# A two-layer decoder on one NeuronCore: loads across two stage borders, a band mask by quadrant products, and a mask by selection with one product on GpSimd

## Chip, cores and metric

One core of one Trainium2 chip runs the whole program, eight stages one after the other in a single launch. The metric is device time in microseconds (us) of one execution. Engines: TensorE (PE), VectorE (DVE), ScalarE (ACT), GpSimd (POOL); SyncE (SP) and ScalarE issue the transfers. Each engine works through its own instruction list in order and waits on semaphores for the others.

## What is computed

Input x is 32 sequences of 128 tokens with 256 features (4,096 tokens), and a context of the same size. Two decoder layers follow. The parts that matter here:

```python
# layer 0, self attention: g = x Wg + bg, v = x Wv + bv, 16 heads of 16
corr = g.g / (|g||g| + 1e-8), masked (j <= i);  corr = (corr + 1) / 2
denom = mean(corr, keys) + 0.5
fitness = 1 / (denom * sum(1 / denom, queries))
p = softmax(corr * fitness where j <= i else -1e10);  x = layernorm(x + (p v) Wo)
# layer 0, cross attention: 16 heads of 16, keys within 64 of the query (the band mask)
# layer 0, feed forward: one quantised 256x256 product
# layer 1, gated attention (Mega): a long convolution over the sequence axis of 32,
#   mx = silu(conv(xn) + omega xn), then attention of 128 queries, 512 values
# layer 1, cross attention: keys and values of width 1,024 from the context
# layer 1: 8 experts, 2 per token
```

## The kernel before, in words

Everything is float32 but for the masks, the identities for them and the quantised product. A tile is 128 tokens, so there are 32 tiles. The stages, with their functions: `l0_attn` (project, then `l0_attn_heads`), `l0_xattn`, `l0_ffn`, `mega_conv`, `mega_attn`, `l1_xattn` and `moe_experts`. A stage ends with all its transfers landed and its semaphores cleared; then all engines begin the next.

**Self attention, heads** (`l0_attn_heads`, lines 237 to 567). Each tile is handled in two halves u = 0, 1 of eight heads. Per tile: GpSimd pads the operands (L318), TensorE transposes them (L448), ScalarE copies them out, TensorE makes correlations and a guard (L461), ScalarE takes a tanh of the guard (L540), VectorE multiplies to the correlation c (L384), GpSimd adds a mask of -1e30 above the diagonal into cm (L324, 327), VectorE sums rows (L400), inverts, TensorE sums the inverses over queries (L477), VectorE makes the fitness (L411) and multiplies cm by it (`weigh`, L393), ScalarE takes the exponential (L546), TensorE transposes it in four groups (L483) that ScalarE copies (L552), TensorE applies it to the values and to ones (L496), VectorE divides (L418), TensorE multiplies by Wo (L514), VectorE adds the residual (L426). The order on each engine is written out by hand: a `walk` over steps s in which each part, with a lag, works on tile s - lag. A wait `slot_free(sem, n, depth)` waits until item n - depth has left the buffer.

**Cross attention of layer 0** (`l0_xattn`, from L569). Groups of four tiles; per tile TensorE first writes the band mask into the score banks (identity times `bandb`, L761: two products of 512 columns per half), then adds the scores (L765), and so on through maximum, exponential, row sum, and a product with the inverse sum on GpSimd (L663) from e into en, which TensorE transposes (L779).

**Keys and values of layer 1** (class `EarlyKeysValues`, L912) depend on the context alone. They are made in 144 pieces, nine per group of two tiles (a transposition of the context, four of keys, four of values), in gaps of the feed forward stage and of the convolution: `make` on TensorE (L957), `keep` on ScalarE (L998). Two banks are used in turn, so a piece waits until the one before the last is kept. In `l0_ffn` one piece stands ahead of the first group (`FFN_FIRST = 1`) and five go with each of eight groups; in `mega_conv` 40 stand ahead of the convolution (`CONV_AFTER`), 8 between its products and the rest behind it. The weights (2 MB) and the first two context loads are issued in `l0_ffn`.

**Convolution** (`mega_conv`). SP loads parameters and xn (L1373), stores the kernel in 32 shifted copies to HBM (`toep`, L1376), waits for these stores, and loads four Toeplitz tiles back (L1381). TensorE multiplies (L1455), ScalarE takes the silu (L1410), SP stores mx (L1385).

**Gated attention** (`mega_attn`). SP first loads group 0 of mx and xn (L1545), then 13 weights and tables (L1558 to 1566). VectorE, ScalarE and TensorE wait for all 13.

## Time and profile before

| what | value |
|---|---|
| median of three runs | 2716.57 us (2715.59 to 2717.06) |
| the profiled execution | 2716.16 us |
| its span | 2714.4 us, 44,490 instructions |
| TensorE busy | 2370.4 us (87%) |
| VectorE busy | 1388.5 us (51%) |
| ScalarE busy | 1126.6 us (42%) |
| GpSimd busy | 874.9 us (32%) |

Busy shares are averages over stages with different limits, so a stage has to be read by itself. PEld is TensorE's loading of the stationary operand, which overlaps its products. In a row of the timeline the bracket tells how long the engine was idle before and what ended it; "issue" means nothing that the profile shows.

### The profile page before, as it was taken

How to read it: one execution, taken by the hardware profiler on the slowest of the kernel's cores; microseconds unless marked ns; L12 is line 12 of the kernel's file. 1: busy time of each engine (PE TensorE's matmuls, PEld its weight loads, DVE VectorE, ACT ScalarE, POOL GpSimd, SP SyncE). 2: the span in 40 equal slices, each digit the busy share in tenths (PEclk: the TensorE clock that was granted, in tenths of full speed). 3: DMA queues.
4: the chain of work that ended last, by engine and by line, in shares of the span. 5: the costliest groups of instructions: out<-in, count | busy, mean ns of one | idle time of the engine just before them, and what ended most of it. 6: DMA issues, size and time to landing. Idle time of an engine off the chain costs nothing. (4 is left out here: it accounts for less than half of the span.)

```text
span 2714.4 us, 44490 instructions
## 1 busy us (share of the span) xinstructions
PE 2370.4 (87%) x17103; PEld 1816.2 (67%) x17134; DVE 1388.5 (51%) x2497; ACT 1126.6 (42%) x1930; POOL 874.9 (32%) x850
## 2 busy tenths in 40 slices
PE   9688888699996668996989959999997799999994
PEld 4466666466664445754656648888886688888883
DVE  5598998477876850002354436877877111111113
ACT  2456666356564544432332315555564111111113
POOL 2455555144444680000010013544544122222221
PEclk9699999899999889997999979999998899999997
DMA  2143444510101649454111032233232766566634
GB/s 74 48 109 105 113 119 114 129 32 24 48 9 36 219 166 242 121 189 130 31 55 39 24 126 86 94 109 122 98 101 88 264 193 180 179 187 193 181 102 136
DMA packets 214465, 313.23 MB, mean 115 GB/s; under 512 B 63856, under 2 KB 196848, under 8 KB 201072
## 3 DMA queue, kind: packets, MB, share of 16 engines
q1 hardware_dynamic: 190992, 253.95, 30.7%
q0 software_dynamic: 14304, 18.69, 3.8%
q10 hardware_dynamic: 8960, 37.75, 3.6%
q8 instruction: 138, 2.26, 0.3%
q14 instruction: 71, 0.58, 0.1%
HBM read 187.58 MB, written 122.76 MB: 114 GB/s over the span
## 5 line engine op out<-in xcount | busy, mean ns | idle before, releaser
L2569 ACT ACTIVATE me_h<-me_ps_h 128x512 f32<-128x512 f32 x156 | 93.1, 597 | 454.1 <-PE me_ps_h L2549 454.1
L2607 DVE TENSOR_SCALAR me_yo<-me_ps_y,moe_xg 128x256 f32<-128x256 f32 x78 | 37.7, 484 | 476.3 <-PE me_ps_y L2558 410.0
L2497 POOL DMA_INDIRECT xo<-me_yo,me_row x78 | 121.8, 1562 | 441.5 <-DVE me_yo L2607 407.3
L2549 PE MATMUL me_ps_h<-me_xt,me_w 128*128 128x256 f32 x1024 | 226.3, 379 | 0.0
L2558 PE MATMUL me_ps_y<-me_w,me_h 128*128 128x256 f32 x1024 | 226.1, 379 | 0.0
L2558 PEld LDWEIGHTS me_ps_y<-me_w,me_h 128*128 128x128 f32 x1024 | 194.6, 190 | 26.5
L2549 PEld LDWEIGHTS me_ps_h<-me_xt,me_w 128*128 128x128 f32 x1024 | 192.1, 190 | 24.8
L327 POOL TENSOR_TENSOR l0ah_cm<-l0ah_c,l0ah_after 128x1024 f32<-128x1024 f32 x64 | 151.7, 2370 | 174.4 <-DVE l0ah_c L389 174.4
L2038 POOL TENSOR_TENSOR l1x_e<-l1x_e,l1x_ri 128x1024 f32<-128x1024 f32 x64 | 121.7, 1901 | 235.4 <-DVE l1x_ri L2322 235.4
L663 POOL TENSOR_TENSOR l0x_en<-l0x_e,l0x_ri 128x1024 f32<-128x1024 f32 x64 | 120.0, 1895 | 208.9 <-DVE l0x_ri L885 208.9
L984 PE MATMUL kv_ps<-kv_w_v,kv_ct 128*128 128x512 f32 x256 | 120.3, 610 | 21.6 <-PEq L82 12.4
L977 PE MATMUL kv_ps<-kv_ct,kv_w_k 128*128 128x256 f32 x512 | 121.8, 395 | 9.5 <-ACT kv_va L1023 6.2
L544 ACT ACTIVATE l0ah_f<-l0ah_ps_s 128x1024 f32<-128x1024 f32 x64 | 65.6, 1025 | 142.8 <-PE l0ah_ps_s L473 142.8
L2157 PE MATMUL l1x_ps_p<-l1x_xct,l1x_w_q 128*128 128x256 f32 x512 | 123.5, 385 | 0.0
L2195 PE MATMUL l1x_ps_o<-l1x_w_o,l1x_ot 128*128 128x256 f32 x512 | 120.4, 389 | 1.4 <-ACT l1x_ot L2268 1.4
L977 PEld LDWEIGHTS kv_ps<-kv_ct,kv_w_k 128*128 128x128 f32 x512 | 100.9, 199 | 30.5 <-ACT kv_va L1023 7.4
L2258 ACT ACTIVATE l1x_e<-l1x_sx 128x1024 f32<-128x1024 f32 x64 | 67.4, 1053 | 115.7 <-DVE l1x_sx L2313 115.6
L844 ACT ACTIVATE l0x_et<-l0x_ps_e 128x512 f32<-128x512 f32 x128 | 69.9, 595 | 99.0 <-PE l0x_ps_e L779 98.7
L1662 DVE TENSOR_SCALAR ma_zq<-ma_zp 128x1 f32<-128x1 f32 x1 | 0.2, 152 | 211.7 <-DMA ma_same<-in_msame 211.7
L2195 PEld LDWEIGHTS l1x_ps_o<-l1x_w_o,l1x_ot 128*128 128x128 f32 x512 | 95.9, 192 | 15.7 <-ACT l1x_ot L2268 1.7
L2319 DVE TENSOR_REDUCE l1x_rs<-l1x_e 128x8 f32<-128x1024 f32 x64 | 78.0, 1219 | 49.0 <-ACT l1x_e L2258 48.5
L2157 PEld LDWEIGHTS l1x_ps_p<-l1x_xct,l1x_w_q 128*128 128x128 f32 x512 | 93.5, 192 | 12.6 <-ACT l1x_xct L2243 0.3
(387 smaller groups left out, 5344.5 us busy)
## 6 DMA issues: line engine op xcount, KB each, us to landing
me_w<-in_w SPq DMA_DIRECT2D x32, 2048.0 KB, 9.5
xs<-dec_zero SPq DMA_DIRECT2D x31, 1032.0 KB, 7.0
k<-kv_kt ACTq DMA_DIRECT2D x16, 1024.0 KB, 6.0
v<-kv_va ACTq DMA_DIRECT2D x16, 1024.0 KB, 6.0
l1x_kt<-k SPq DMA_DIRECT2D x16, 1024.0 KB, 4.9
l1x_va<-v SPq DMA_DIRECT2D x16, 1024.0 KB, 5.6
moe_w_first<-in_w SPq DMA_DIRECT2D x7, 2048.0 KB, 10.3
moe_xg<-xs SPq DMA_DIRECT2D x39, 258.0 KB, 2.8
```

What stands on the lines that cost most here:

```text
L327: pool.tensor_tensor(cm[:, n % 2, u, :, :], c[:, u, :, :], after[:, :].unsqueeze(1).to_broadcast([P, HALF, P]), ALU.add).then_inc(corr_mas ...
L663: pool.tensor_tensor(en[:, n % 2, u, :, :], e[:, n % 2, u, :, :], spread(ri[:, n % 2, u, :], P), ALU.mult).then_inc(e_scaled, 1)
L977: ins = pe.matmul(bank[:, c * self.GP:(c + 1) * self.GP], self.w_k[:, k, at], self.ct[:, g % 2, k, :], start=k == 0, stop=k == 1)
L984: ins = pe.matmul(bank[:, :], self.ct[:, g % 2, k, t * P:(t + 1) * P], self.w_v[:, k, 512 * c:512 * c + 512], start=k == 0, stop=k == 1)
L2038: pool.tensor_tensor(e[:, n % 2, u, :, :], e[:, n % 2, u, :, :], spread(ri[:, n % 2, u, :], P), ALU.mult).then_inc(e_scaled, 1)
L2157: last = pe.matmul(ps_p[i % 2][:, c * GP:(c + 1) * GP], w_q[:, k, at], xct[:, k, :], start=k == 0, stop=k == 1)
L2195: last = pe.matmul(ps_o[:, 0:2, :].rearrange("p a b -> p (a b)"), ot[:, c, :], w_o[:, c, :], start=c == 0, stop=c == C - 1)
L2319: dve.tensor_reduce(rs[:, n % 2, u, :], e[:, n % 2, u, :, :], AX.X, ALU.add).then_inc(summed, 1)
L2497: pool.indirect_dma_start(token_rows, bass.IndirectOffsetOnAxis(row[:, j % 2, q:q + 1], 0), yo[:, j % 2, q, :], None, compute_op=ALU.add). ...
L2549: last = pe.matmul(ps_h[i % HB][:, f % 2, :], weights(j)[:, FFN * c + f * P:FFN * c + f * P + P], xt[:, j % 2, c, :], start=c == 0, stop=c ...
L2558: last = pe.matmul(ps_y[q][:, 0:D], h[:, j % 2, f, q * P:(q + 1) * P], weights(j)[:, W2 + D * f:W2 + D * f + D], start=f == 0, stop=f == F ...
L2569: act.activation(h[:, j % 2, 2 * i:2 * i + 2, :], ps_h[i % HB][:, :, :], ACT.Gelu).then_inc(gelued, 1)
```

## The change

Self attention: the mask is no longer added to c. The product with the fitness reads c itself; the exponential is made without a mask, and GpSimd then sets it to zero above the diagonal, in place, with two selects per tile. The product for u = 1 moves from VectorE to GpSimd, which gets its fitness from a buffer fs of its own. The order on all engines is new. Cross attention: the band is added behind the scores, only where it can be nonzero, by products of 64 rows, 64 output partitions and 4 x 64 columns; the product with the inverse sum is made in place. The key and value weights and first contexts are loaded in the cross attention; ten pieces stand ahead of the feed forward's first group. The gated attention's weights and its first xn are loaded within the convolution, between the stores of `toep` and the loads of the Toeplitz tiles, and its first mx at that stage's end. Some of its tiles are laid over buffers of `EarlyKeysValues`.

```diff
@@ l0_attn_heads, GpSimd
-                def mask_corr(n, u):
-                    item_done(pool, corr_done, 2 * n + u)
-                    slot_free(pool, weighted, 2 * n + u, 4)
-                    pool.tensor_tensor(cm[:, n % 2, u, :, :], c[:, u, :, :], after[:, :].unsqueeze(1).to_broadcast([P, HALF, P]),
-                                       ALU.add).then_inc(corr_masked, 1)
+                def weigh_odd(n):
+                    item_done(pool, fit_done, n)
+                    item_done(pool, corr_done, 2 * n + 1)
+                    slot_free(pool, exped, n, 1, 2)
+                    pool.tensor_tensor(wt[:, 1, :, :], c[:, n % 2, 1, :, :], spread(fs[:, n % 2, :], P), ALU.mult).then_inc(weighted1, 1)
+
+                def mask_e(n, u):
+                    item_done(pool, exped, 2 * n + u)
+                    pool.affine_select(out=e[:, n % 2, u, :, :], in_=e[:, n % 2, u, :, :], compare_op=ALU.is_ge, fill=0.0, base=0,
+                                       pattern=[[0, HALF], [-1, P]], channel_multiplier=1).then_inc(masked, 1)
-                walk([(4, last_of_group(roots)), (3, bias_x), (0, lambda n: mask_corr(n, 0)), (-1, pads), (0, lambda n: mask_corr(n, 1))])
+                walk([(-2, pads), (1, lambda n: mask_e(n, 0)), (1, lambda n: mask_e(n, 1)), (2, last_of_group(roots)), (0, bias_x), (0, weigh_odd)])
@@ l0_attn_heads, VectorE
-                def weigh(n, u):
-                    i = 2 * n + u
+                def weigh_even(n):
                     item_done(dve, fit_done, n)
-                    item_done(dve, corr_masked, i)
-                    slot_free(dve, exped, i, 2)
-                    dve.tensor_tensor(wt[:, u, :, :], cm[:, n % 2, u, :, :], spread(small(3)[:, HALF * u:HALF * u + HALF], P), ALU.mult).then_inc(weighted, 1)
+                    slot_free(dve, exped, n, 1, 2)
+                    dve.tensor_tensor(wt[:, 0, :, :], c[:, n % 2, 0, :, :], spread(small(3)[:, 0:HALF], P), ALU.mult).then_inc(weighted0, 1)
-                walk([(0, lambda n: correlate(n, 0)), (3, residual), (1, lambda n: weigh(n, 0)), (1, lambda n: weigh(n, 1)), (0, lambda n: correlate(n, 1)), (0, row_sums),
-                      (2, divide), (0, fitness)])
+                walk([(1, weigh_even), (0, lambda n: correlate(n, 1)), (2, divide), (0, row_sums), (2, residual), (-1, lambda n: correlate(n, 0)), (0, fitness)])
@@ l0_attn_heads, TensorE
-                    item_done(pe, exped, 2 * n + j // 2)
+                    item_done(pe, masked, 2 * n + j // 2)
-                walk([(3, multiply), (0, lambda n: score(n, 1)), (2, lambda n: transpose_e(n, 0)), (2, lambda n: transpose_e(n, 1)),
-                      (2, lambda n: transpose_e(n, 2)), (2, lambda n: transpose_e(n, 3)), (-1, transposes), (2, apply), (-1, lambda n: score(n, 0)),
-                      (0, sum_inverse)])
+                walk([(3, multiply), (2, lambda n: transpose_e(n, 0)), (1, sum_inverse), (2, lambda n: transpose_e(n, 1)), (2, lambda n: transpose_e(n, 2)), (2, lambda n: transpose_e(n, 3)), (0, lambda n: score(n, 1)), (2, apply), (-1, transposes), (-1, lambda n: score(n, 0))])
@@ l0_attn_heads, ScalarE
-                walk([(0, lambda n: guard(n, 1)), (2, copy_et), (7, normalise), (-1, copy_ops), (1, lambda n: exponentials(n, 0)),
-                      (1, lambda n: exponentials(n, 1)), (-1, lambda n: guard(n, 0))])
+                walk([(0, copy_ops), (2, lambda n: exponentials(n, 1)), (0, lambda n: guard(n, 0)), (7, normalise), (2, copy_et), (0, lambda n: guard(n, 1)), (1, lambda n: exponentials(n, 0))])
@@ l0_xattn, GpSimd: the product in place, ScalarE's wait
-                        pool.tensor_tensor(en[:, n % 2, u, :, :], e[:, n % 2, u, :, :], spread(ri[:, n % 2, u, :], P),
+                        pool.tensor_tensor(e[:, n % 2, u, :, :], e[:, n % 2, u, :, :], spread(ri[:, n % 2, u, :], P),
-                    slot_free(act, e_scaled, n, 2, 2)
+                    slot_free(act, e_transposed, n, 2, 4)
@@ l0_xattn, SP
+                    if g + 3 == NG:
+                        kv.load_weights(sp)
+                        for early in range(2):
+                            kv.load_ctx(sp, early)
@@ l0_xattn, TensorE, score
-                        for q in range(2):
-                            pe.matmul(ps_s[u][:, q, :, :], identb[:, :], bandb[:, :, :], start=True, stop=False)
                         for c in range(2):
                             for q in range(2):
                                 at = slice(32 * (2 * u + q), 32 * (2 * u + q) + 32)
-                                last = pe.matmul(ps_s[u][:, q, 2 * c:2 * c + 2, :], qt[at, g % 2, c, t * P:(t + 1) * P],
-                                                 kt[at, g % 2, c, :, t * P:(t + 1) * P], start=False, stop=c == 1)
+                                pe.matmul(ps_s[u][:, q, 2 * c:2 * c + 2, :], qt[at, g % 2, c, t * P:(t + 1) * P],
+                                          kt[at, g % 2, c, :, t * P:(t + 1) * P], start=c == 0, stop=False)
+                        for q in range(2):
+                            for lo in range(2):
+                                rows64, keys64 = slice(64 * lo, 64 * lo + 64), slice(64 - 64 * lo, 128 - 64 * lo)
+                                last = pe.matmul(ps_s[u][rows64, q, :, keys64], identb[rows64, rows64], bandb[rows64, :, keys64],
+                                                 start=False, stop=True)
@@ l0_ffn
-FFN_FIRST, FFN_STEP = 1, 5
+FFN_FIRST, FFN_STEP = 10, 5
-                kv.load_weights(sp)
...
-                for g in range(2):
-                    kv.load_ctx(act, g)
...
+                kv.keep(act, 0, 2)
                 sum_squares(0)
                 act.wait_ge(w_loaded, 5 * 16)
                 act.activation(w[:, :, :], w_i[:, :, :], ACT.Copy).then_inc(w_ready, 1)
-                kv.keep(act, 0, FFN_FIRST)
+                kv.keep(act, 2, 5)
                 sum_squares(1)
+                kv.keep(act, 5, FFN_FIRST)
@@ mega_conv, SP
                                  kp[:, :, L - 1 - l:2 * L - 1 - l]).then_inc(pad_stored, 16)
+                mw.load_weights(sp)
+                mw.load(sp, 0, xn, 0)
                 sp.wait_ge(pad_stored, 16 * L)
...
                 sp.wait_ge(stored, 16 * G)
+                mw.load(sp, 1, mx_out, 0)
@@ mega_attn, SP: load(0) and the 13 weight loads are gone; tiles over the buffers of kv
+        v = kv.kt[:, :, :, :].rearrange("p u (t c) n -> p u t (c n)", t=G)
+        r = kv.va[:, :, :, :].rearrange("p u t (c n) -> p u (t c) n", c=2)
+        hr = kv.w_kv[:, :, :, :].rearrange("p u k (c m n) -> p u (k c) m n", c=2, m=4)
```

## Rows read from the trace of the kernel before

**Rows 1.** Busy time by stage, columns as headed.

```profile
core 0: us, PE busy (x) PEld busy (x) DVE busy (x) ACT busy (x) POOL busy (x), PEclk, DMA share, GB/s
...
72.00:500.00 428.00, 342.12 (x5312) 268.33 (x5312) 353.23 (x454) 245.53 (x358) 217.24 (x237) 0.93 0.42 106
500.00:879.00 379.00, 336.79 (x2657) 218.54 (x2688) 275.96 (x323) 207.73 (x338) 153.44 (x112) 0.97 0.12 38
```

**Rows 2.** Timeline (start us, us, engine, line), self attention, about one tile.

```profile
303.29 0.54 PEld L467 LDWEIGHTS l0ah_ps_s<-l0ah_ops 16*128 16x128 f32 x16 [0.20 <-issue]
...
305.15 0.40 PE L481 MATMUL l0ah_ps_a<-l0ah_st,l0ah_ones 128*128 128x16 f32 x2
...
305.29 1.02 ACT L544 ACTIVATE l0ah_f<-l0ah_ps_s 128x1024 f32<-128x1024 f32 x1 [0.70 <-PE l0ah_ps_s L473]
...
306.34 1.22 DVE L389 SCALAR_TENSOR_TENSOR l0ah_c<-l0ah_f,l0ah_ps_s 128x1024 f32<-128x1024 f32 x1 [0.28 <-ACT l0ah_f L544]
...
308.50 2.35 DVE L398 TENSOR_TENSOR l0ah_wt<-l0ah_cm,l0ah_ps_a 128x1024 f32<-128x1024 f32 x2
...
311.37 1.12 PE L493 MATMUL l0ah_ps_e<-l0a_ident,l0ah_e 128*128 128x128 f32 x8 [0.70 <-ACT l0ah_et L556]
...
312.02 2.29 DVE L402 TENSOR_REDUCE l0ah_st<-l0ah_c 128x16 f32<-128x2048 f32 x1
...
313.29 0.65 PE L504 MATMUL l0ah_ps_e<-l0ah_et,l0a_va 128*32 128x128 f32 x16
...
314.55 0.26 DVE L409 RECIPROCAL l0ah_st<-l0ah_ps_a 128x16 f32<-128x16 f32 x1
...
315.31 1.76 DVE L421 RECIPROCAL l0ah_rd<-l0ah_ps_e 128x256 f32<-128x256 f32 x1 [0.50 <-PE l0ah_ps_e L510]
...
317.10 0.42 DVE L424 TENSOR_TENSOR l0ah_ot<-l0ah_ps_e,l0ah_rd 128x256 f32<-128x256 f32 x1
...
318.22 1.22 DVE L389 SCALAR_TENSOR_TENSOR l0ah_c<-l0ah_f,l0ah_ps_s 128x1024 f32<-128x1024 f32 x1 [0.28 <-ACT l0ah_f L544]
```

**Rows 3.** Timeline, cross attention: from one tile's multiply to its transposes.

```profile
645.16 0.73 PEld L800 LDWEIGHTS l0x_ps_e<-l0x_w_o,l0x_ot 128*128 128x128 f32 x4 [0.20 <-issue]
...
647.71 0.11 PEld L761 LDWEIGHTS l0x_ps_s<-l0x_bandb,l0x_identb 128*128 128x128 bf16 x2 [0.33 <-issue]
...
648.25 0.73 PEld L765 LDWEIGHTS l0x_ps_s<-l0x_kt,l0x_qt 32*128 32x128 f32 x8 [0.42 <-issue]
...
649.31 0.86 PEld L779 LDWEIGHTS l0x_ps_e<-l0x_ident,l0x_en 128*128 128x128 f32 x8 [0.33 <-issue]
```

**Rows 4.** Timeline, feed forward: its first transposes and VectorE's first residual.

```profile
897.03 1.01 PE L1239 MATMUL ffn_ps_t<-ffn_identb,ffn_xq 128*128 128x128 bf16 x8 [11.91 <-DVE ffn_xq L1289]
...
904.15 1.65 DVE L1298 SCALAR_TENSOR_TENSOR ffn_r<-ffn_ps_y,ffn_st,ffn_xb 128x256 f32<-128x256 f32 x4
```

**Rows 5.** Timeline, gated attention: its first loads, copies and projection.

```profile
1222.55 2.85 SPq L1545 DMA_DIRECT2D ma_xin<-mx  x4
...
1234.93 0.47 SPq L1566 DMA_DIRECT2D ma_same<-in_msame  x1
...
1242.25 1.08 ACT L1603 ACTIVATE ma_xt<-ma_ps_t 128x512 f32<-128x512 f32 x2 [24.82 <-DMA ma_same<-in_msame]
...
1245.74 3.78 PE L1807 MATMUL ma_ps_z<-ma_xt,ma_w_z 128*128 128x512 f32 x4 [0.38 <-DVE ma_bm L1679]
```

**Rows 6.** Groups of instructions on GpSimd: busy us, mean ns, idle before.

```profile
L327 POOL TENSOR_TENSOR l0ah_cm<-l0ah_c,l0ah_after 128x1024 f32<-128x1024 f32 x64 | 151.7, 2370 | 174.4 <-DVE l0ah_c L389 174.4
...
L663 POOL TENSOR_TENSOR l0x_en<-l0x_e,l0x_ri 128x1024 f32<-128x1024 f32 x64 | 120.0, 1895 | 208.9 <-DVE l0x_ri L885 208.9
```

**Rows 7.** The same view, a select on GpSimd.

```profile
L642 POOL TENSOR_SCALAR_AFFINE_SELECT l0x_band<-l0x_band 128x512 f32<-128x512 f32 x1 | 0.6, 641 | 0.1
```

**Rows 8.** Timeline, convolution: its first product, and pieces of keys behind it.

```profile
1084.61 3.84 PE L1455 MATMUL mc_ps<-mc_xg,mc_t 128*128 128x128 f32 x16 [6.33 <-DMA mc_t<-toep]
...
1173.40 7.07 PE L977 MATMUL kv_ps<-kv_ct,kv_w_k 128*128 128x256 f32 x32
...
1188.13 7.07 PE L977 MATMUL kv_ps<-kv_ct,kv_w_k 128*128 128x256 f32 x32
```

More of the change, by code:

```diff
@@ L922, in __init__ @@
         self.ident = kit.sb("ident", [P, P])
[L923 removed]
+        self.w_kv = kit.sb("w_kv", [P, 2, 2, H * self.W])
+        self.w_k, self.w_v = self.w_kv[:, 0, :, :], self.w_kv[:, 1, :, :]
         self.b_k = kit.sb("b_k", [P, self.C])
@@ L928, in __init__ @@
         self.va = kit.sb("va", [P, 2, self.G, H * self.W])
-        self.ps = [kit.ps(f"ps{i}", [P, 2 * self.GP]) for i in range(2)]
         self.k_loaded, self.v_loaded = kit.sem("k_loaded"), kit.sem("v_loaded")
@@ L935, in __init__, with take_banks @@
         self.kit = kit
+    def take_banks(self, kit):
+        self.ps = [kit.ps(f"ps_kv{i}", [P, 2 * self.GP]) for i in range(2)]
     def piece(self, n):
@@ L1525, in mega_attn @@
          normed) = (kit.sem(n) for n in names)
-        xin_loaded = [[kit.sem(f"{c}_loaded{u}") for u in range(2)] for c in ("xn", "mx")]
         x_loaded = [kit.sem(f"x_loaded{u}") for u in range(3)]
@@ L1542, in load @@
                     slot_free(sp, xt_ready, g, 2, 4)
-                    for c, src in ((1, mx_in), (0, xn_in)):
-                        for t in range(G):
-                            sp.dma_start(xin[:, g % 2, c, t, :], tiles(src)[G * g + t, :, :, :]).then_inc(xin_loaded[c][g % 2], 16)
+                    mw.load(sp, 1, mx_in, g)
+                    mw.load(sp, 0, xn_in, g)
                 def load_x(g):
```

131 lines of the change are left out of this document (73 added, 58 removed).

## The prediction

> **What bounds the kernel now.** I read the stage windows first, because the 44,490 instructions fall into stages that run one after the other, then the timeline of one period inside each stage that the diff touches, then the borders. In the self attention's head stage VectorE is busy 353 of 428 us and TensorE 342; in the cross attention TensorE is busy 337 of 379 and VectorE 276 [rows 1]. So the first is a cycle between engines with VectorE as its fullest member, the second runs at TensorE's order. The reader is to see in the timeline that one tile of the head stage takes 318.22 - 306.34 = 11.88 us [rows 2]. In the cross attention the same TensorE steps repeat with idle gaps of 0.2 to 0.4 us, the longer ones at a change of matmul form [rows 3]. At the borders two idle stretches stand out: TensorE sits 11.9 us before the first transposes of the FFN [rows 4], and the gated attention, though its first input has landed, starts its copies only at 1242.25, when the last of 13 weight loads has landed, 24.8 us after ScalarE went idle [rows 5].
>
> **Sum is made against the profiled execution:** 2716.16 us, with a span of 2714.4; the median of the runs is 2716.57, so 0.4 more. 0.2% is 5.4 us, about what a measurement of this kernel can tell from no change.
>
> **Self attention, heads.** Removed: two GpSimd additions of 2.37 us per tile and the copy cm; one VectorE product (two take 2.35 us) goes to GpSimd [rows 2, 6]. Added on GpSimd: one product of the same form as the cross attention's, 1.90 us [rows 6], and two selects over 128x1024 in place. The trace has a select over 128x512, 0.64 us [rows 7]; twice that, 1.28, is my value, with 0.64 and 2.37 (the addition, same size) as ends. GpSimd's sum for these falls from 4.74 to 1.90 + 2.56 = 4.46 us of 11.9: it is on no bound. VectorE falls from 353/32 = 11.0 to about 10 us a tile, but what closes the period is the new order, so I walked it. From TensorE's sum of inverses: that product 0.40; one group of four transposes 0.55; its bank's copy before the last group may start, about 0.75 (the row shows 0.70 of such idle); the last group 0.5; together 2.2. The score of half u=1, until tanh starts: 305.29 - 303.29 = 2.00. Tanh, until the correlation starts: 306.34 - 305.29 = 1.05. The correlation 1.22, less 0.07 overlap. Divide, which now stands ahead of the row sums: 317.10 - 315.31 + 0.42 = 2.2 (its input, the apply product, takes 315.31 - 313.29 = 2.02 after the score and is ready by then). Row sums until the inverse is there: 314.55 + 0.26 - 312.02 = 2.79. Signal back to TensorE 0.13. Sum 11.5 us, against 11.88: 0.38 x 32 tiles = **-12 us** [rows 2]. GpSimd is not in this cycle, nor is the moved product: the even product (1.2) and the odd one run beside the score. Ends: TensorE's own 342/32 = 10.7 us a tile would give -38; a tenth of a microsecond missed in the walk's other direction, with the gain gone, +3. The earlier addition of x and bias has a load issued a whole tile ahead, so I cost it at nothing; a late load would hold GpSimd's queue, the odd product with it, and GpSimd has 11.5 - 4.46 - 2.0 = 5 us of room a tile, so only what passes those counts.
>
> **Cross attention.** Per half the band's two 512-column products take 648.25 - 647.71 = 0.54 us, loads and streaming; a half's score takes 649.31 - 648.25 = 1.06 before another form may start; and a tile's multiply, band, score take 647.71 - 645.16 = 2.55 [rows 3]. Afterwards four 256-column products per half stand behind the score. Streaming alone is 0.54 - 0.11 = 0.43 for 1,024 columns, so 0.107 for each product of 256. If the two diagonal quadrants of one pair run side by side, a half's band is 0.21 plus 0.11 to 0.2 of load and drain, 0.33 to 0.42. Multiply then changes straight to the narrow form, 0.73 + 0.33. A tile is 1.06 + 2 x 1.06 + 2 x 0.37 = 3.9 against 649.31 - 645.16 = 4.15: 0.22 x 32 = **-7 us** (ends -4 and -10). TensorE's order is the bound, so this passes through; VectorE has 3 us of room a tile. The product in place on GpSimd changes no duration, and ScalarE's new wait on the transposes is already met, as the same engine copies those banks earlier in the same step. Two megabytes of key and value weights and two context loads are issued here now, behind the last input load, with nothing but stores behind them: 0; without cover it would be one store a few microseconds late, with two buffers of four tiles to absorb it.
>
> **FFN head.** Nine more pieces of keys and values are made before the first group. Nine pieces (one group of two tiles) take 1188.13 - 1173.40 = 14.73 us [rows 8]. They fill the 11.9 us idle and the start moves forward by the context load that is no longer waited for. The first transposes come some 4 us later, yet VectorE takes up the first product only at 904.15, after its own work, with no idle before it [rows 4]; that leaves room, which I put at 2 to 3 us. I take **0** (-1 to +3).
>
> **Convolution.** Nine pieces leave its tail, which TensorE bounds: -14.7 [rows 8]. Against that, SP now issues 13 weight loads and 4 loads of xn before the four loads of the Toeplitz tiles. In the gated attention 8 input and 13 weight loads took 1234.93 + 0.47 - 1222.55 = 12.85 us to issue, 0.61 each, so 17 take 10.4 [rows 5]; about 1 of it lies in the wait for its stores that SP has there in any case: +9.4. TensorE already waits 6.3 us for these tiles [rows 8], so the whole delay shows. The 3.4 MB also go ahead of the tiles in the same queue: there, 3.9 MB were in after 1242.25 - 1222.55 = 19.7 us, so 3.4 MB would take 17, most of it beside the issue. Ends +6 and +17. Stage: -14.7 + 9.4 = **-5.3**. The stores of mx move with it and have 46 pieces, 46 x 14.73 / 9 = 75 us, behind them as cover; uncovered, they would give back the rest of the 14.7.
>
> **Gated attention.** Its 13 weights, xn and mx of group 0 have landed. The stage's first instruction is at 1222.55; identity, four groups of transposes with their copies, and the small products need about 5.9 us, so its first projection starts at about 1228.4 instead of 1245.74: -17.3 [rows 5]. The 5.9 is 1245.74 - 1242.25 = 3.5 from the first copy on, plus the first two groups of transposes and the identity, which used to lie in the wait. Some of the first products also leave the slow clock earlier, so **-18** (-16 to -20). The tiles borrowed from the keys' buffers are written after those stores were waited for. One more clearing of semaphores: +0.4.
>
> **Sum:** -12 - 7 + 0 - 5.3 - 18 + 0.4 = -41.9: 2716.2 - 41.9 = **2674 us**.
>
> **Rivals.**
> *The quadrants do not run side by side.* Both write one bank, while the scores' two row groups q, which the kernel of before runs as a pair, go to separate banks. Then a half's band is 0.43 + 0.11 to 0.2, a tile 1.06 + 2.12 + 1.2 = 4.35 against 4.15: +6 instead of -7, so 2687. The Trainium skill, TensorEngine Tiling (Array Packing), section Restrictions and Gotchas, says that different row tiles cannot access the same PSUM bank simultaneously; by it this rival holds. No run here shows it. What speaks for overlap is that the pairs differ in output partitions too. Chance 0.3.
> *The weights delay the Toeplitz tiles further.* If the 3.4 MB drain at their old pace and the tiles follow only then, beside the keys' stores, the convolution starts 17 to 23 us late instead of 9.4, about 20: 2685. For: the 19.7 us above. Against: SP's issue overlaps the drain, and the keys' traffic stops once TensorE idles. Chance 0.1. The Trainium skill, DMA: Bandwidth & Descriptors, section Queues, rings and completion order, says that each engine takes a row's descriptors in ring order; with that the drain is in front, not beside.
> *The head stage's order closes tighter*, near TensorE's 10.7: 2650 to 2660. Against: the walk above. Chance 0.07.
> *Slower: GpSimd becomes the bound of the head stage.* Its place: two selects a tile ahead of the odd product on one in-order engine. With s for a select, its tile is 2s + 1.90 + 2.0 of other work (217/32 - 4.74) [rows 1, 6]. It decides above s = 3.8 us, where that passes 11.5; the whole gain is spent at about s = 4.45. At s = 5 the tile is 13.9: 2.4 x 32 = +77 on the sum: 2751. Against: 0.64 us for half the size [rows 7]. Chance 0.03.
> *It doesn't do what it says:* TensorE's first projection still waits, for mx of group 0 or another load: the 18 are lost: 2692. The load of mx is issued after its stores, with tens of microseconds of pieces behind. Chance 0.03.
> The forecast, as summed, has 0.47.
>
> **How the numbers follow.** The likeliest case alone spans 2665 to 2683. To leave out no more than 2 in 10 the range takes in the serial quadrants and the later tiles with their ends, and the tighter order in part: 2656 to 2697. Faster by over 0.2% (below 2711) is every case but the GpSimd bound and a pile of bad ends: 0.94; same 0.03; slower 0.03.
>
> **What would show it.** Head stage: period near 11.5 us, divide ahead of the row sums, selects near 1.3 us. Cross attention: the gap from a half's score to the next form, near 0.37 or 0.6. Convolution: its idle before the first product near 16 us instead of 6.3, its tail 14.7 shorter. Gated attention: first projection 6 us after the stage's start. A head stage not faster, or TensorE idle for over 25 us ahead of the convolution, would make the prediction wrong.

## The result, and the profile after

The changed kernel takes 2681.57 us in the median of four executions (2678.93 to 2689.17), the kernel before 2716.08: a ratio of 0.9876, with a 95% interval of 0.9859 to 0.9893, or 34.5 us less. The forecast was 2674, with a range of 2656 to 2697, and 0.94 for faster by over 0.2%. The profiled execution is the longest of the four, 2689.17 us with a span of 2687.4. Against the profiled execution before (2716.16) it gained 27.0 us, and the stages below account for those 27.0, not for the median's 34.5.

Busy time by stage in the profile after; columns as headed, and a stage runs from its own first instruction to the next one's.

```profile
core 0: us, PE busy (x) PEld busy (x) DVE busy (x) ACT busy (x) POOL busy (x), PEclk, DMA share, GB/s
80.30:506.30 426.00, 355.55 (x5312) 277.30 (x5312) 308.00 (x448) 252.46 (x355) 197.25 (x270) 0.90 0.41 107
506.30:878.30 372.00, 331.32 (x2816) 219.45 (x2816) 275.97 (x323) 207.96 (x338) 153.59 (x113) 0.96 0.14 46
878.30:1010.20 131.90, 99.37 (x424) 66.68 (x425) 93.33 (x233) 73.40 (x180) 94.68 (x109) 0.90 0.55 193
1010.20:1221.60 211.40, 183.07 (x664) 125.85 (x664) 5.43 (x11) 87.69 (x157) 7.14 (x4) 0.94 0.71 189
1221.60:1564.70 343.10, 297.54 (x1282) 205.93 (x1282) 156.08 (x290) 113.38 (x168) 27.73 (x29) 0.98 0.15 47
```

| stage | before, start to start | after | change | forecast |
|---|---|---|---|---|
| self attention, heads | 421.3 | 426.0 | +4.7 | -12 |
| cross attention | 378.3 | 372.0 | -6.3 | -7 |
| feed forward | 130.5 | 131.9 | +1.4 | 0 |
| convolution | 212.3 | 211.4 | -0.9 | -5.3 |
| gated attention | 368.7 | 343.1 | -25.6 | -18 |

The later stages are as before within 0.5 us. Stage by stage, the profiled execution gained 15 us less than the forecast 41.9: the head stage is 16.7 us longer than forecast and the convolution 4.4, while the gated attention gained 7.6 us more than it should. Two large errors work against each other, and the median, 7.6 us below the profiled execution, lies nearer to the forecast than these stages do.

**The head stage's period is the one that was walked out.** Timeline of one tile after, the rows that answer to [rows 2]:

```profile
306.92 0.40 PE L486 MATMUL l0ah_ps_a<-l0ah_st,l0ah_ones 128*128 128x16 f32 x2 [0.64 <-DVE l0ah_st L412]
...
309.25 0.73 PE L472 MATMUL l0ah_ps_s<-l0ah_ops 16*128 16x128 f32 x16
...
311.25 1.02 ACT L547 ACTIVATE l0ah_f<-l0ah_ps_s 128x1024 f32<-128x1024 f32 x1 [1.29 <-PE l0ah_ps_s L478]
...
312.30 1.22 DVE L394 SCALAR_TENSOR_TENSOR l0ah_c<-l0ah_f,l0ah_ps_s 128x1024 f32<-128x1024 f32 x1 [1.68 <-POOL l0ah_wt L328]
...
313.44 1.75 DVE L427 RECIPROCAL l0ah_rd<-l0ah_ps_e 128x256 f32<-128x256 f32 x1
...
315.56 2.28 DVE L405 TENSOR_REDUCE l0ah_st<-l0ah_c 128x16 f32<-128x2048 f32 x1
...
318.09 0.26 DVE L412 RECIPROCAL l0ah_st<-l0ah_ps_a 128x16 f32<-128x16 f32 x1
...
318.40 0.40 PE L486 MATMUL l0ah_ps_a<-l0ah_st,l0ah_ones 128*128 128x16 f32 x2 [0.64 <-DVE l0ah_st L412]
```

From one sum of inverses to the next it is 318.40 - 306.92 = 11.48 us. The walk's seven steps measure: transposes 2.33 us (forecast 2.2), score 2.00, tanh 1.05 and row sums to inverse 2.79 (all three as forecast), correlation 1.14 (forecast 1.15), divide 2.12 (forecast 2.2), and signal 0.05 (forecast 0.13). The bracket at 312.30 names GpSimd's product, whose end falls there by chance: the same product of the next tile ends at 322.83, and that tile's correlation starts only at 323.78, when its tanh is done.

**And yet the stage is longer**, because five of its tiles are much longer. In each, TensorE stands still in the middle of a run of transposes. TensorE's products at one of these places:

```profile
275.40 0.27 PE L463 MATMUL l0ah_ps_a<-l0a_ident,l0ah_rpad 128*128 128x128 f32 x1
275.51 0.27 PE L462 MATMUL l0ah_ps_a<-l0a_ident,l0ah_lpad 128*128 128x128 f32 x1
278.27 0.33 PE L463 MATMUL l0ah_ps_a<-l0a_ident,l0ah_rpad 128*128 128x128 f32 x1 [2.48 <-issue]
...
281.57 2.08 PE L525 MATMUL l0ah_ps_e<-l0ah_w_o,l0ah_ot 128*128 128x256 f32 x4
```

The same stretch by engine, four microseconds each:

```profile
272.00:276.00 4.00, 3.78 (x95) 2.87 (x91) 2.33 (x3) 2.17 (x3) 2.93 (x5) 1.00 1.09 275
276.00:280.00 4.00, 1.48 (x22) 1.12 (x23) 3.97 (x3) 1.37 (x3) 0.62 (x1) 1.00 0.08 16
280.00:284.00 4.00, 4.00 (x29) 3.07 (x28) 0.84 (x4) 2.17 (x3) 1.09 (x1) 0.58 0.00 0
```

The reader should see three things. The product at 278.27 carries no wait ("issue"), and its twin at 275.40 ran without pause. The DMA engines are full (share 1.09) in the 4 us ahead: a zero store of 1 MB was issued at 270.66. And behind the gap the granted clock falls to 0.58, near the lower level of 1.2 GHz, so that the output product takes 2.08 us instead of the 1.13 that it takes elsewhere. The five tiles take 13.7, 14.4, 14.8, 15.1 and 16.6 us from row sums to row sums instead of 11.49, standstill and slow clock together. (One more, near the stage's start, takes 13.6 us with no gap: there the granted clock is at the lower level until 116.8 us.) The kernel before has no such gap in this stage; behind its first tiles only two are stretched, by 1.1 us each.

**Cross attention, convolution, gated attention.** The quadrants in the cross attention, after:

```profile
641.08 0.14 PEld L773 LDWEIGHTS l0x_ps_s<-l0x_bandb,l0x_identb 64*64 64x64 bf16 x4 [0.33 <-issue]
641.42 0.86 PEld L787 LDWEIGHTS l0x_ps_e<-l0x_ident,l0x_e 128*128 128x128 f32 x8 [0.20 <-issue]
```

A half's band takes 641.42 - 641.08 = 0.34 us, where [rows 3] had 0.54. SP's loads at the border, the convolution's first product, and the first two projections of the gated attention, after:

```profile
1072.09 0.47 SPq L950 DMA_DIRECT2D mw_w_z<-in_mwz  x1
...
1081.79 3.69 SPq L964 DMA_DIRECT2D mw_xin<-xn  x4
...
1085.61 8.15 SPq L1441 DMA_DIRECT2D mc_t<-toep  x4
...
1098.13 2.07 PE L1516 MATMUL mc_ps<-mc_xg,mc_t 128*128 128x128 f32 x8 [19.70 <-DMA mc_t<-toep]
...
1226.86 1.98 PE L1843 MATMUL ma_ps_z<-ma_xt,mw_w_z 128*128 128x512 f32 x4 [0.39 <-DVE ma_bm L1715]
...
1256.54 1.88 PE L1843 MATMUL ma_ps_z<-ma_xt,mw_w_z 128*128 128x512 f32 x4
```

The 17 loads hold SP for 1085.61 - 1072.09 = 13.5 us, and TensorE now waits 19.7 us for the Toeplitz tiles, where [rows 8] had 6.33 and the forecast near 16. The gated attention's first projection starts 5.3 us after the stage, as against 23.2 [rows 5].

### The profile page after: what moved, and what is told of

The parts are those of the page before. It is cut to its first block and busy times, and to the rows that moved or that the text cites. A ratio compares the mean times of both kernels' runs of the same rounds, so it can differ in the third digit from the quotient of the medians.

```text
span 2687.4 us, 44698 instructions
## 1 busy us (share of the span) xinstructions
PE 2370.5 (88%) x17262; PEld 1822.0 (68%) x17262; DVE 1349.1 (50%) x2497; ACT 1136.7 (42%) x1930; POOL 855.7 (32%) x882
## 5 line engine op out<-in xcount | busy, mean ns | idle before, releaser
L664 POOL TENSOR_TENSOR l0x_e<-l0x_e,l0x_ri 128x1024 f32<-128x1024 f32 x64 | 120.1, 1897 | 201.7 <-DVE l0x_ri L893 201.7
L394 DVE SCALAR_TENSOR_TENSOR l0ah_c<-l0ah_f,l0ah_ps_s 128x1024 f32<-128x1024 f32 x64 | 77.2, 1207 | 74.9 <-ACT l0ah_f L547 66.5
L1043 PE MATMUL mc_ps_kv<-kv_w_kv,kv_ct 128*128 128x512 f32 x176 | 83.3, 616 | 16.8 <-PEq L82 14.0
L332 POOL TENSOR_SCALAR_AFFINE_SELECT l0ah_e<-l0ah_e 128x1024 f32<-128x1024 f32 x64 | 69.9, 1094 | 87.8 <-ACT l0ah_e L553 87.2
L2346 DVE TENSOR_REDUCE l1x_top<-l1x_ps_s 128x8 f32<-128x1024 f32 x64 | 77.6, 1213 | 39.4 <-PE l1x_ps_s L2204 38.5
L559 ACT ACTIVATE l0ah_et<-l0ah_ps_e 128x512 f32<-128x512 f32 x128 | 73.7, 596 | 54.1 <-PE l0ah_ps_e L498 53.2
```

The lines of the kernel that those rows point to most:

```text
L394: dve.scalar_tensor_tensor(out=c[:, n % 2, u, :, :].rearrange("p (r g) k -> p r g k", g=2), in0=f[:, u, :, :].rearrange("p (r g) k -> p r ...
L664: pool.tensor_tensor(e[:, n % 2, u, :, :], e[:, n % 2, u, :, :], spread(ri[:, n % 2, u, :], P), ALU.mult).then_inc(e_scaled, 1)
L1043: ins = pe.matmul(bank[:, :], self.ct[:, g % 2, k, t * P:(t + 1) * P], self.w_v[:, k, 512 * c:512 * c + 512], start=k == 0, stop=k == 1)
L2346: dve.tensor_reduce(top[:, u, :], scores, AX.X, ALU.max).then_inc(maxed, 1)
```

## The experiments

The runs were made in three sets of four, in the order of their names below: `again`, `heads_alone`, `zeros_in_cross`, `tiles_first`; `shift_after`, `shift_before`, `zeros_early`, `band_full`; `borders_alone`, `select_twice`, `inverse_twice`, `ffn_one`. Each set had a chip of its own, where the kernel before had a median of 2713.0, 2713.8 and 2713.5 us. "The changed kernel" stands below for its median in the first of these sets.

### The change again, and the head stage alone

The first is the changed kernel unedited; the second is the kernel before with the changed `l0_attn_heads` and nothing else.

> The changed kernel itself, once more. Theory S: in the head stage TensorE stands still, with no wait to end it, each time its own instruction list has passed another 1,024 instructions just behind a burst of the 1 MB zero stores; the places are fixed in the program, so the five stalls of 2 to 3 us come back inside the runs of transposes (L462, L463) at the same instructions, and the stage again takes near 424 us instead of the 32 x 11.49 that its period gives. Rival R: the five stalls were an accident of that one execution (2689 against 2679 to 2683 in the others); then the stage takes about 409 us and the profile's time is near 2672.

> The kernel before with the new self attention head stage alone. Theory S: the period is 11.49 us instead of 11.88 as in the changed kernel (-12 us over 32 tiles), but stalls of the instruction stream and the slow clock behind them cost about 13 to 18 us, so the kernel is within 6 us of the kernel before, on either side. Rival R (no stalls, the prediction's sum holds): 12 us faster, about 2704.

The changed kernel took 2685.77 us (2679.35 to 2692.22), ratio 0.9891 (0.9872 to 0.9909). The head stage took 424.3 us in its profile, and gaps of over 2 us came back at five places, four of them the same as in the first profile; at the fifth of the first profile TensorE stood for 1.0 us. So they are no accident; S holds, R falls.

The head stage alone is worth nothing, as S had it: 2714.6 us (2708.52 to 2727.54), ratio 1.0001 (0.9991 to 1.0011), in place of the 12 us of its period. Its profiled execution, its slowest, shows seven such gaps and a head stage of 433.1 us.

Counted in TensorE's own list (loads, products and semaphore instructions), the gaps of all these profiles stand at a number that leaves 451 when divided by 1,024: 1,475, 3,523, 4,547, 5,571, 7,619, 8,643 or 9,667. A tile has 342 such instructions, and three tiles 1,026, so every third tile these places fall almost at the same point of the new order, behind a zero store. One queue of the trace (8, kind "instruction") moves 139 packets of 16,384 bytes; for TensorE's 35,711 instructions that is 64 bytes apiece and 256 instructions a packet, so 1,024 instructions are four packets. (The kernel before, with 35,422 instructions, has 138 packets there.)

### Zero stores elsewhere

```diff
@@ l0_attn_heads, SP
-                unrolled(TILES, [(0, load), (1, clear), (8, store)])
+                unrolled(TILES, [(0, load), (8, store)])
@@ l0_xattn, SP, in the loop over groups, behind store(g - 1)
+                    for n in range(ZERO_PARTS // NG * g, ZERO_PARTS // NG * (g + 1)):
+                        clear(n)
```

> The changed kernel, with its 32 zero stores of 1 MB issued in the cross attention (four per group of tiles) instead of one per tile in the self attention. Theory S: the stalls of 2 to 3 us in the head stage go, or shrink below 1 us, and the stage falls from 424 to about 408 us; the cross attention, whose transfers were busy 0.14 of the time, pays 0 to 5 us. Total 8 to 18 us faster than the changed kernel. Rival F (the stalls belong to the place in the instruction list whatever the transfers do): the five stalls stay, the stage stays at 424 us, the total within 3 us of the changed kernel.

2694.22 us, 8 slower than the changed kernel, where 8 to 18 faster was expected. The stages say what happened:

```profile
80.20:484.30 404.10, 341.20 (x5312) 266.47 (x5312) 307.20 (x448) 251.57 (x355) 196.77 (x270) 0.94 0.08 24
484.30:883.30 399.00, 331.32 (x2816) 219.44 (x2816) 275.93 (x323) 207.83 (x338) 153.47 (x113) 0.93 0.57 132
```

The head stage is 404.1 us, 20 less than in the repeated run, with a period of 11.48 to 11.49 on every steady tile but one (11.73 us), and no gap is left. F falls: without the stores' traffic the same instructions run through. The cross attention lost 27 instead of 0 to 5. The queue shows where (its DMA issues, same kernel):

```profile
847.79 11.39 SPq L698 DMA_DIRECT2D xs<-dec_zero  x4
859.23 12.61 SPq L683 DMA_DIRECT2D x<-l0x_y  x1
883.27 0.37 SPq L1159 DMA_DIRECT2D ffn_x<-x  x1
```

The stage's last store stood behind the last zeros, and the feed forward began at 883. The loss was one of placing, which the next runs mend.

### The place in the list moved, the transfers left

```diff
@@ l0_attn_heads, TensorE, ahead of the walk (64 in the changed kernel, 100 in the kernel before)
                 pe.wait_ge(identb_set, 1)
+                for _ in range(64):
+                    pe.matmul(ps_a[0][:, 0, 0:16], identb[:, :], identb[:, 0:16], start=True, stop=True)
```

> The changed kernel with 64 products of 16 columns more ahead of the head stage's first transposes, which compute nothing that is read: they move every later place in TensorE's list by 128 instructions, and leave the order, the transfers and their timing as they are. Theory S: TensorE stops only where the 1,024th instruction falls 4.4 to 5.3 us behind the start of a 1 MB zero store; moved 128 instructions (about a third of a tile, 4 us) forward, that point falls within 1 us of the burst's start, the stalls in L462 and L463 go, the head stage falls from 422 to 424 us to 403 to 409, and the total is 12 to 20 us less than the changed kernel (about 2668). Rival P (the stall belongs to the transposes behind a burst, not to the place in the list): still four or more stalls of 2 to 3 us in the transposes, total unchanged or 3 us longer.

> The kernel before, with 100 such products more. Its zero stores start 9.3 to 11.8 us ahead of the places in question; moved 200 instructions (some 7 us) forward these fall 3.5 to 5 us behind a burst's start. Theory S: the kernel before gets stalls of 2 to 3 us too, at several of the ten places, and its head stage grows by 10 to 20 us (2723 to 2733). Rival P: no new stalls, at most 4 us for the products themselves.

With the 64 products the changed kernel took 2672.88 us (2668.94 to 2674.69), ratio 0.985 (0.9837 to 0.9862): 12.9 less than without them. TensorE's loads waiting for "issue" in the head stage, in us in total, times, longest; first the changed kernel:

```profile
PEld l0ah_ps_a L462 <- issue: 26.0, 31, 14.6
PEld l0ah_ps_a L463 <- issue: 7.5, 3, 2.9
```

then with the 64 products, where those two lines are L464 and L465:

```profile
PEld l0ah_ps_a L464 <- issue: 5.8, 29, 0.2
```

No gap is left in the transposes; 0.2 us each is the usual start of that run of transposes, and the changed kernel's 14.6 is the wait at the stage's start. The stage took 407.6 us from start to start instead of 424 to 426, under the same stores. P falls: the stop goes with the place in the list, not with the transposes. But six shorter stops, of 0.6 to 1.1 us, now stand in the scores, and two tiles take 13.3 and 13.4 us. One of the six, in TensorE's products:

```profile
247.46 0.60 PE L477 MATMUL l0ah_ps_s<-l0ah_guardb,l0ah_identb 128*128 128x256 bf16 x4 [1.13 <-issue]
```

The converse failed. The kernel before with 100 products took 2714.09 us (ratio 0.9998, 0.999 to 1.0007), and its head stage 421.3 as ever: no gap, though the places stood 3.0 to 5.8 us behind the issue of a zero store, much like the 4.4 to 5.1 of the five gaps after. So a store just ahead of such a place isn't enough.

**What else it takes stands in the traces: each stop is the wait for a late packet of TensorE's own instructions.** The five stops of the first profile, with the transfer (on queue 8) of the packet of instructions that begins there, in us (the profile names no such wait; it is read from these times):

| place in the list | last start ahead of the stop | packet starts | packet has landed | TensorE goes on |
|---|---|---|---|---|
| 3,523 | 201.73 | 200.97 | 202.22 | 203.72 |
| 4,547 | 238.29 | 238.33 | 239.60 | 240.94 |
| 5,571 | 275.51 | 275.80 | 277.01 | 278.26 |
| 7,619 | 347.44 | 347.86 | 349.19 | 350.44 |
| 8,643 | 385.27 | 385.97 | 387.13 | 388.48 |

TensorE goes on 1.25 to 1.50 us after the landing, and in none of the 14 traces does it start a packet's first instruction sooner than 1.19 us after it. Where nothing stopped, the packet was early: 4.3 and 6.2 us ahead at 1,475 and 9,667 in the same profile, which also stood 5.2 and 4.4 us behind a store; at least 2.4 us ahead throughout the kernel before, and 1.85 in the same kernel with its 100 products. The six short stops of the changed kernel with 64 products end 1.2 to 1.5 us behind a landing too, at 1,986, 5,058, 6,082, 7,106, 9,154 and 10,178. These leave 962, which is two packets on from 450, the weight load of the product at 451. So the remainder is no property of the list: which of the four packets in three tiles comes late depends on where they fall. And the stores make it late: at 4,547, with the same instructions, the packet started its transfer when TensorE had none left in the changed kernel, 5.0 us behind the issue of a store, and when it had 251 left with the stores in the cross attention. In `tiles_first`, with the stores in place, that packet came ahead of the store, with 251 left, and nothing stopped there. What decides when a packet's transfer begins was not found: with the stores gone most begin with 200 to 260 instructions left, but one with 140.

### Both moves together

```diff
@@ mega_conv, SP
-                mw.load_weights(sp)
-                mw.load(sp, 0, xn, 0)
                 sp.wait_ge(pad_stored, 16 * L)
                 sp.wait_ge(t_zeroed, 1)
                 for g in range(G):
                     sp.dma_start(t[L * g:L * g + L, :, L * g:L * g + L],
                                  toep[:, CH * g:CH * g + CH, :]).then_inc(t_loaded, 16)
+                mw.load_weights(sp)
+                mw.load(sp, 0, xn, 0)
@@ l0_xattn, SP (second kernel only, with the stores taken out of l0_attn_heads)
+                    for n in range(6 * g, min(6 * g + 6, ZERO_PARTS)):
+                        clear(n)
```

> The changed kernel, with the four loads of the Toeplitz tiles issued ahead of the 13 weight loads and the four of xn. Theory: the convolution's first product came 13.5 us later than before because SP issued 17 loads first; with the tiles first it starts near 1085 again, the tail of key pieces keeps its gain of 14.7 us, and the weights, landed over 100 us before their use, cost the gated attention nothing: 12 to 14 us faster than the changed kernel. Rival: the weights' 3.4 MB beside the tiles' stores or the mx stores delay something else (mx stores landing after the last piece): less than 5 us.

> The changed kernel with both moves: the Toeplitz tiles loaded ahead of the gated attention's weights, and the 32 zero stores issued in the cross attention, now six to a group in the first groups so that none is left for the last two. Theory: the head stage ends near 482 us as in the run with four to a group, the cross attention and its border take 374 us as in the changed kernel (the 19 us that it lost with four to a group were its last stores and the weights waiting behind the last zeros), and the tiles give 13 to 15 us: 2648 to 2655 in all. Rival: 6 MB in a group hold up the loads of the next groups and the stage loses more than 8 us.

Tiles first: 2670.29 us (2668.82 to 2675.49), 15.5 less than the changed kernel, where 12 to 14 was expected. The edit's own part is the 12 us in the stage below; the head stage, which it doesn't touch, was 3.7 us shorter in this profile than in the second. Its first product in the convolution, from its timeline, and the stage:

```profile
1081.56 3.83 PE L1516 MATMUL mc_ps<-mc_xg,mc_t 128*128 128x128 f32 x16 [8.06 <-DMA mc_t<-toep]
```

```profile
1004.70:1204.30 199.60, 182.91 (x664) 125.80 (x664) 5.43 (x11) 87.64 (x157) 7.11 (x3) 0.96 0.74 200
```

The wait for the tiles is 8.06 us instead of 19.7, and the stage is 11.8 shorter than in the first profile after (12.5 than in the second). The gated attention keeps its gain (345.9), so the weights' early place bought nothing.

With the zeros early as well: 2653.4 us (2652.14 to 2660.99), ratio 0.979 (0.9775 to 0.9805), 60 below the kernel before and the lowest median of all. Its stages from the self attention to the convolution:

```profile
81.30:483.10 401.80, 338.41 (x5312) 264.72 (x5312) 307.22 (x448) 251.75 (x355) 197.18 (x269) 0.95 0.08 25
483.10:854.60 371.50, 330.57 (x2816) 218.62 (x2816) 275.99 (x323) 207.88 (x338) 153.60 (x112) 0.96 0.61 142
854.60:986.20 131.60, 100.40 (x424) 66.88 (x424) 93.38 (x233) 73.62 (x180) 94.66 (x109) 0.89 0.56 193
986.20:1186.00 199.80, 183.51 (x664) 125.97 (x664) 5.43 (x11) 87.69 (x157) 7.11 (x3) 0.96 0.74 199
```

The head stage is 24 us shorter than in the first profile after, and the cross attention, with 33 MB of zeros in it, takes what it took without them.

### The parts by themselves

```diff
@@ l0_xattn, TensorE, score: as before, in the place of the quadrants
+                        for q in range(2):
+                            pe.matmul(ps_s[u][:, q, :, :], identb[:, :], bandb[:, :, :], start=True, stop=False)
```

> The changed kernel with the cross attention's band mask written as before, two products of 512 columns per half ahead of the scores. Theory (the quadrants of a pair run side by side): the period goes from 10.85 back to 11.14 us per tile, 0.29 x 32 = 9 us slower than the changed kernel, 6 to 9 by the stage's length. Rival (quadrants one after the other, the gain only in the order of forms): 0 to 3 us slower.

2697.96 us (2684.72 to 2699.96), 12 above the changed kernel; 372.0 us of stage became 380.0, which is the band's part, and the head stage of this profile has six stops instead of five. A half's band and what follows it, in its timeline:

```profile
652.25 0.11 PEld L766 LDWEIGHTS l0x_ps_s<-l0x_bandb,l0x_identb 128*128 128x128 bf16 x2 [0.33 <-issue]
652.79 0.73 PEld L770 LDWEIGHTS l0x_ps_s<-l0x_kt,l0x_qt 32*128 32x128 f32 x8 [0.42 <-issue]
```

A half's band takes 0.54 us here and 0.34 with the quadrants. Four products of 256 columns one after the other would stream for 0.43 us by the forecast's own price, and the whole band took less than that, so they overlap: in the trace the two products of a pair, which write one bank, start 4 ns apart. The Trainium skill, TensorEngine Tiling (Array Packing), section Restrictions and Gotchas, states that different row tiles can't access one PSUM bank simultaneously; the measured 0.34 us speaks against it for tiles that differ in output partitions too.

The borders alone (the changed kernel with the head stage and the band mask of before):

> The kernel before with the loads across the two borders (and the piece order and buffers that go with them) alone: head stage and band mask are as before. Theory, by the stages of the changed kernel's profile: feed forward +1, convolution -1 (its tail 14.7 shorter, its start 13.5 later), gated attention -19 from its loads and 0 to -7 from fewer slow stretches of the clock: 17 to 27 us faster than before. With 0 for the head stage alone and 9 to 12 for the band this adds up to the change's 30. Rival (the parts help each other): less than 14 or over 30.

2693.3 us (2690.82 to 2693.68), ratio 0.9923 (0.9909 to 0.9937): 20 us. That is within the 17 to 27 expected. So the parts are 0, 12 and 20 by their medians, from three sets, and add up to 32; the changed kernel measured 27 in the set of `again` and 34.5 in the first result. Its gated attention:

```profile
1225.20:1568.70 343.50, 297.75 (x1282) 206.04 (x1282) 156.07 (x290) 113.39 (x168) 27.61 (x28) 0.98 0.16 46
```

So neither the head stage nor the quadrants bring the extra gain there. One piece ahead of the feed forward instead of ten, on top of the run with both moves:

```diff
-FFN_FIRST, FFN_STEP = 10, 5
+FFN_FIRST, FFN_STEP = 1, 5
```

> The same run, with one piece of keys and values ahead of the feed forward's first group instead of ten. Theory (the nine pieces ran in TensorE's idle time before the first transposes): the feed forward is 1 to 3 us shorter, the convolution's tail 14.7 us longer: 11 to 14 us slower in all. Rival (the convolution's end is set by the stores of mx, not by the pieces): 0 to 5 us slower.

2671.06 us, 17.7 slower (expected 11 to 14). The stages:

```profile
861.20:992.40 131.20, 84.41 (x372) 57.00 (x373) 93.28 (x233) 67.83 (x167) 94.57 (x109) 0.85 0.51 176
992.40:1206.10 213.70, 197.35 (x716) 135.38 (x716) 5.44 (x11) 93.94 (x170) 7.14 (x4) 0.97 0.72 198
1206.10:1554.60 348.50, 302.97 (x1282) 208.11 (x1282) 155.99 (x290) 113.38 (x168) 27.79 (x29) 0.96 0.15 46
```

The pieces cost the feed forward 0.4 us (131.6 against 131.2) and gave the convolution 13.9; the forecast had 0 and 14.7. The gated attention, which was not touched, is 5.5 longer at a granted clock of 0.96 instead of 0.98, and the head stage 408.9 instead of 401.9: that is the spread in which such a comparison stands.

### Is GpSimd in the cycle, and is the walked cycle one?

On top of the run with both moves, each select a second time, or the 0.26 us reciprocal behind the row sums a second time, into buffers that nothing reads:

```diff
+                    pool.affine_select(out=again[:, :, :], in_=e[:, n % 2, u, :, :], compare_op=ALU.is_ge, fill=0.0, base=0,
+                                       pattern=[[0, HALF], [-1, P]], channel_multiplier=1)
@@ the other kernel, VectorE, row_sums
+                    dve.reciprocal(flat(again[:, :, :]), small(1))
```

> The run with the tiles first and the zeros early, with each of the 64 selects done a second time (into a buffer that nothing reads), 1.09 us each, 2.2 us of GpSimd more per tile of the head stage. Theory (GpSimd is not in the cycle, and half 1's probabilities are waited for about 1.5 us later than they are ready): the period stays at 11.49 us, the total within 3 us. Rival (GpSimd or the select is in the cycle): 1.1 to 2.2 us a tile, 35 to 70 us slower.

> The same run, with the 0.26 us reciprocal behind the row sums done a second time into a buffer that nothing reads. Theory (the walk: divide, row sums, inverse, sum over queries on TensorE, transposes, score, tanh, correlation are one closed cycle): the period rises by the whole 0.2 to 0.26 us to about 11.72, 6 to 8 us in all. Rival (TensorE's or another order closes the period): it stays at 11.49.

Two selects more a tile cost nothing: 2653.51 us against 2653.4 (of the set before), period 11.48 to 11.49. In its timeline the last select of a tile starts at 306.40 and takes 1.09 us; the transposes that need it come at 308.34, 0.85 later:

```profile
306.40 1.09 POOL L337 TENSOR_SCALAR_AFFINE_SELECT l0ah_e<-l0ah_e 128x1024 f32<-128x1024 f32 x1
...
308.34 1.07 PE L495 MATMUL l0ah_ps_e<-l0a_ident,l0ah_e 128*128 128x128 f32 x8
```

The second reciprocal lengthens every period, to 11.59 or 11.60, and the total is 2658.89 us, 5.5 more. In its timeline:

```profile
308.28 0.26 DVE L405 RECIPROCAL l0ah_again<-l0ah_ps_a 128x16 f32<-128x16 f32 x1
308.45 0.19 DVE L406 RECIPROCAL l0ah_st<-l0ah_ps_a 128x16 f32<-128x16 f32 x1
308.70 0.40 PE L480 MATMUL l0ah_ps_a<-l0ah_st,l0ah_ones 128*128 128x16 f32 x2 [0.75 <-DVE l0ah_st L406]
...
320.29 0.40 PE L480 MATMUL l0ah_ps_a<-l0ah_st,l0ah_ones 128*128 128x16 f32 x2 [0.75 <-DVE l0ah_st L406]
```

The two overlap, so the inverse is ready (308.45 + 0.19) - (308.28 + 0.26) = 0.10 us later, not 0.26, and the period grows by just that, 320.29 - 308.70 = 11.59 against 11.48. What was mis-sized was the probe; what it tells stands: a tenth of a microsecond on that chain goes into the period in full, and 2.2 us on GpSimd don't.

## Why the prediction was right where it was, and wrong where it was not

**The total.** 2681.6 lies 7.6 us from the forecast and within the likeliest case's own 2665 to 2683. The gain was 34.5 us against 42, and part of the nearness is luck: the head stage's lost gain was partly made up by one in the gated attention that no term had, as the points below show.

**Head stage: the term -12 failed.** The walk is right to 0.02 us (11.48 for 11.5), GpSimd is outside it as stated, and a select of 128x1024 took 1.09 us (forecast 1.28). The step that failed is "0.38 x 32 tiles": it took the steady period for the whole stage. TensorE's stops for late instruction packets and the slow clock behind them took back all of it: 12.9 us by the run with moved places, where short stops remain, and some 20 by the head stages of the profiles with and without the stores (424.3 against 404.1). The forecast had no case for this. It spoke of the period "near 11.5" as the sign that would prove the stage, and of "a head stage not faster" as one that would make the prediction wrong. Both came true: 11.48 us, and a stage of 426.0 us against 421.3. By its own words the prediction was wrong in this stage, though not in the total.

**Cross attention: right, by size and reason.** Multiply, bands and scores of a tile take 652.28 - 648.43 = 3.85 us (forecast 3.9, before 4.15); the stage gained 6.3 in the profile, 8.0 against its own counterpart, forecast -7 (-4 to -10). The rival with serial quadrants (chance 0.3, +6) fell.

**Feed forward: right.** +1.4 in the profile within -1 to +3, though the run with one piece puts only 0.4 of it on the pieces.

**Convolution: the term +9.4 was mis-sized.** The tail gained its 14.7, but the tiles came 1098.13 - 1084.61 = 13.5 us later. The mechanism (17 issues ahead of the tiles on SP) was the one named, and the tiles took as long from their issue to TensorE's start as before (1098.13 - 1085.61 = 12.5; before they were issued at 1072.19, 12.4 ahead of 1084.61). Wrong was the size of an issue, 0.61 us from [rows 5]: here 17 took 13.5, 0.80 each. It isn't a matter of which loads they are, for in `tiles_first` the same 17 took 10.3 us, 0.61 each, behind the tiles; why they are slower right behind the stores of `toep` was not found. The wait for those stores did hide more than the 1 us taken off (it was 1.6 us before), but the 32 stores themselves took 32.0 us to issue instead of 30.3, which no term had. The rival of a longer delay (17 to 23 us) didn't come true.

**Gated attention: the term -18 was right and not the whole.** From the stage's start to the first projection it is 5.3 us instead of 23.2, -17.9 (the forecast had 5.9). Between the first and the second projection another 1.9 went with the slow clock at the start: 1277.37 - 1245.74 = 31.6 before, where the granted clock is at the lower level until 1249.7 us, and 29.7 after, where it is so only until 1226.1, ahead of the first projection. The other 6 were in no term. Before, the projections from the third group on stand 42.7 us apart in some groups; after, 41.03. From the timeline before:

```profile
1315.55 1.88 PE L1807 MATMUL ma_ps_z<-ma_xt,ma_w_z 128*128 128x512 f32 x4
...
1358.27 1.88 PE L1807 MATMUL ma_ps_z<-ma_xt,ma_w_z 128*128 128x512 f32 x4
```

and after, the same two groups:

```profile
1294.72 1.88 PE L1843 MATMUL ma_ps_z<-ma_xt,mw_w_z 128*128 128x512 f32 x4
...
1335.75 1.88 PE L1843 MATMUL ma_ps_z<-ma_xt,mw_w_z 128*128 128x512 f32 x4
```

In the profile before, four groups carry about 1.6 us each of that kind, and each of the four holds one stretch of 3.4 us at the lower level (0.91 in 20 us there); after, it is 1.00 from the second 20 us on. The stage took 368.7, 362.2 and 368.9 us in the three profiles without the borders' change, with four, one and four such dips, and 343 to 349 in all with it, with none in seven and one to three in four of them. So the dips differ from execution to execution of like stages, and the 6 us can't all be put down to the borders. Why the clock dips in the one and not in the other was not settled.

## What to carry to other kernels

A period read from a steady tile bounds a stage from below; multiply it by the tiles only after the stage's length before has been checked against its own period, and look in the new profile for the tiles that are longer. Large stores that nobody waits for are not free of charge beside a TensorE with many small instructions, because its instructions come through the same DMA engines: put them into a stage whose TensorE runs few and long ones, and not into its last groups. And where TensorE stands with "issue" among equal instructions, look for a packet of its instructions that lands just ahead of the point where it goes on. And loads brought forward belong behind those that the stage itself waits for: here the order of two lines on SP was worth 12 us of the convolution.

## What the runs showed of the hardware that was not expected

TensorE can stop for 1 to 3.5 us in the middle of a row of equal instructions with no wait in the profile, because the packet with its next 256 instructions (16,384 bytes) is late. It goes on 1.2 to 1.5 us after the packet has landed, in all 29 stops of over 1 us of the five profiles that have the changed head stage, its stores and no added products. The packet is late when a 1 MB store fills the DMA engines (share 1.09) at the time: its transfer then starts 3.5 to 5.4 us behind the issue of the store. Behind each of the five stops of the first profile the granted clock is at the lower level for 3.4 or 6.8 us (0.58 over 4 us at one). With the stores gone, stops of this size are gone; with the place in the list moved, other packets were late, and by less.

Two quadrants of 64 rows and 64 output partitions that write one bank overlap: their products start 4 ns apart, and four products of 256 columns take 0.34 us. Two small reciprocals (128x16) in a row overlap too: the second ends 0.10 us after the first, though it takes 0.19.
